# A fused group-norm, channel-attention and box-count kernel: the orders of five engines' half chunks rewritten, VectorE's operations of two units interleaved

## The reference, cut to what matters

```python
# layer 0
x = x + _L0_conv_ref(_gn(x), gamma)     # channel attention: softmax(x^T x), applied to x
# layer 1, on v = _gn(x), scaled to its own least and greatest value
measures = stack([box_sum(v, k) for k in (2, 4, 8, 16)])
log_m    = log(measures + EPS)
alphas   = slope of log_m over log(k)
excite   = sigmoid(relu(mean(alphas) @ w1 + b1) @ w2 + b2)
sim      = cosine of log_m (centred) and the fitted line (centred)
out      = x + sim * sigmoid(batch_norm(alphas)) + (1 - sim) * v * excite
```

## Time and profile before

| | |
|---|---|
| median of 3 runs | 6843.75 us (6843.52 to 6863.24) |
| profiled execution | 6870.93 us, span 6869.2 us |
| busy share of the span: VectorE, TensorE, ScalarE, GpSimd | 80%, 74%, 70%, 26% |
| 32 half chunks of turn 6, first to last L963 | 693.6 us |
| TensorE's mean granted clock | 0.907 of 2.4 GHz |

### The profile page before, as it was taken

The page is one execution under the profiler, slowest core; times in us unless marked ns, Lnnn a source line. Parts: engine busy times, 40 slices in busy tenths (PEclk is TensorE's granted clock), DMA queues, the critical chain, the costliest instruction groups (busy, mean ns, idle before and its releaser), DMA issues. The chain is left out here.

```text
span 6869.2 us, 108733 instructions
## 1 busy us (share of the span) xinstructions
PE 5112.8 (74%) x35320; PEld 4647.5 (68%) x35320; DVE 5524.0 (80%) x6453; ACT 4827.6 (70%) x5203; POOL 1757.7 (26%) x1201
## 2 busy tenths in 40 slices
PE   6968886788858888588867888588885777466643
PEld 6757776677747777477766777477774666466642
DVE  1359998689969999699986999689996999699961
ACT  0118887588848888488875888488884888588861
POOL 0022221422232222322213222322223222333310
PEclk9989998899979999799988999799997999788875
DMA  3635554577746777477755777467774666456656
GB/s 117 195 114 166 176 171 130 176 232 240 230 148 214 226 232 230 132 235 230 223 190 169 238 241 228 148 208 228 236 230 126 219 221 220 159 170 187 189 176 230
DMA packets 874516, 1344.69 MB, mean 196 GB/s; under 512 B 38705, under 2 KB 694097, under 8 KB 857937
## 3 DMA queue, kind: packets, MB, share of 16 engines
q1 hardware_dynamic: 837456, 1208.16, 51.7%
q0 software_dynamic: 36864, 134.23, 10.3%
HBM read 671.16 MB, written 536.87 MB: 176 GB/s over the span
## 5 line engine op out<-in xcount | busy, mean ns | idle before, releaser
L530 PE MATMUL even<-band,t 128*128 128x128 f32 x12288 | 1867.0, 283 | 473.9 <-ACT logs L706 293.3
L530 PEld LDWEIGHTS even<-band,t 128*128 128x128 f32 x12288 | 1625.7, 197 | 548.6 <-issue 444.4
L387 POOL TENSOR_TENSOR t<-t 128x1024 f32<-128x1024 f32 (+3 forms) x800 | 1337.3, 1683 | 1451.3 <-DVE logs L979 1408.3
L511 PE MATMUL h_ps<-mix,xt 128*128 128x256 f32 x4096 | 1054.6, 403 | 454.0 <-DVE mx L891 327.3
L511 PEld LDWEIGHTS h_ps<-mix,xt 128*128 128x128 f32 x4096 | 773.8, 199 | 603.0 <-ACT xt L693 310.7
L428 POOL DMA_DIRECT2D x1t<-logs x256 | 226.4, 884 | 2882.9 <-DVE ut L990 2815.4
L706 ACT ACTIVATE logs<-even,col 128x1024 f32<-128x1024 f32 x512 | 568.8, 1111 | 444.6 <-PE even L530 443.2
L532 PE MATMUL even<-band,t 128*128 128x128 f32 x4096 | 792.0, 275 | 0.0
L891 DVE CUSTOM_DVE_ANT_0 h_out<-h_ps,shift,mx 128x512 f32<-128x512 f32 x512 | 382.7, 748 | 488.5 <-PE h_ps L511 487.5
L488 PE MATMUL g_ps<-xa 128*128 128x257 f32 x2048 | 634.8, 391 | 152.4 <-DMA xa<-in_x_dram 152.1
L532 PEld LDWEIGHTS even<-band,t 128*128 128x128 f32 x4096 | 621.9, 192 | 0.0
(11 more groups left out here) (184 smaller groups left out, 10492.4 us busy)
## 6 DMA issues: line engine op xcount, KB each, us to landing
xa<-in_x_dram SPq DMA_DIRECT2D x256, 512.0 KB, 4.5
xb<-in_x_dram SPq DMA_DIRECT2D x256, 512.0 KB, 5.5
h_scratch<-h_out SPq DMA_DIRECT2D x128, 1024.0 KB, 7.7
hr<-h_scratch SPq DMA_DIRECT2D x256, 512.0 KB, 6.0
q_scratch<-ut SPq DMA_DIRECT2D x256, 512.0 KB, 2.7
x1t<-logs POOLq DMA_DIRECT2D x256, 512.0 KB, 5.1
p_scratch<-x1t SPq DMA_DIRECT2D x256, 512.0 KB, 3.1
pd<-p_scratch SPq DMA_DIRECT2D x256, 512.0 KB, 6.1
```

Of the source, the lines that this page charges most:

```text
L387: ins = g.tensor_tensor(dst[:, hf, d:d + n, :], src[:, hf, d:d + n, :], src[:, hf, e:e + n, :], ALU.add)
L511: ins = t.matmul(h_ps[:, r * C:(r + 1) * C], xt[:, q % 2, jh, r, :], mix[:, jh, :], start=(jh == 0), stop=(jh == 1))
L530: ins = t.matmul(o, src[:, hf, at, :], band[:, which, :], start=True, stop=(which < 3))
```

## The change

Five edits, all in the order of operations or in what they wait for; no operation is added or removed.

1. SyncE: `load_rows` goes ahead of the stores of h and of the output.
2. TensorE: the second `gram_rows` goes from before `box` 3 to behind `turn_back` 0, ahead of the second `mix_x`.
3. ScalarE: order log 0, `copy_xt`, log 2, two squares, log 1, third square, Exp, log 3.
4. VectorE: `norms`, `contrasts` and `finish` are cut into single operations. Each waits for its own producer's count (`dve_done` value handed from one to the other) instead of for the last operation issued. Their order in a half chunk is below.
5. `copy_h` no longer waits for its own end; it waits for the end of the `copy_h` before it, and `min_h` waits for the `copy_h` that it reads. `copy_h` 2 goes behind `high_contrast`; `row_pairs` ahead of the last operation of the tail; `add_slopes` to the next half chunk.

```diff
 # SyncE half_chunk
                     sp.dma_start(pd[:, hf, :], p_dram[ud]).then_inc(pq_loaded[hf], 16)
                     sp.dma_start(qd[:, hf, :], q_dram[ud]).then_inc(pq_loaded[hf], 16)
+                if Cs and not (began and hf == 0) and not (last and (k, hf) != (0, 0)):
+
+                    sp.wait_ge(odd_filled, 2 * u)
+                    apart()
+                    if hf == 1:
+                        load_rows(nC + 2, 1 - k, 0)
+                    else:
+                        load_rows(nC + 1, k, 1)
                 if Bs and hf == 0 and not began:
...
 # TensorE half_chunk
-                if A:
-                    gram_rows(n, hf, 1)
                 if Cs:
                     box(u, k, hf, 3)
...
                 if Ds:
                     turn_back(2 * nd + hf, hf, 0)
+                if A:
+                    gram_rows(n, hf, 1)
                 if Bs:
                     mix_x(nb, 2 * hf + 1)
...
 # VectorE half_chunk
+                v, vf = u - 1, 1 - hf
+                if tail:
+                    two = two_squares(v, vf)
                 if Ds:
                     p_plus_q(nd, 2 * nd + hf, hf)
                 if tail:
-                    norms(u - 1, 1 - hf)
+                    three = three_squares(v, vf, two)
+                if Cs and hf == 0 and tail:
+                    add_slopes(v, 1 - k)
+                if tail:
+                    norm(v, vf, three)
                 if Bs:
                     copy_h(nb, k, 2 * hf, first, 16 * (8 * (s - 1) + i))
                 if Cs:
-                    low_contrasts(u, hf)
+                    low = low_contrasts(u, hf)
+                    high_contrast(u, hf)
                 if Bs:
                     copy_h(nb, k, 2 * hf + 1, first, None)
                 if Cs:
-                    high_contrast(u, hf)
+                    summed = sum_contrast(u, nC, hf, low)
                 if Bs:
-                    min_h(i, k, hf)
-                if Cs:
-                    contrasts(u, nC, k, hf)
+                    min_h(nb, i, k, hf)
                 if tail:
-                    finish(u - 1, 1 - hf)
-                if Cs and hf == 1:
-                    add_slopes(u, k)
+                    similar = similarity(v, vf)
+                if Cs:
+                    cubed = cubic(u, hf, summed)
+                    quadratic(u, hf)
+                    linear(u, k, hf, cubed)
+                if tail:
+                    made = product(v, vf, similar)
...
                 if Cs and not (last and k == 1):
                     row_pairs(k, hf, 16 * (8 * (s - 2) + i + 2), last)
+                if tail:
+                    gated(v, vf, made)
```

More of the change, by code:

```diff
@@ L887, in copy_h @@
                 dve.wait_ge(h_filled, m + 3)
+                dve.wait_ge(h_copied, m + 1)
                 if q == 0 and some(stored):
@@ L939, in low_contrasts @@
                 d.tensor_tensor(L[0], L[0], odd[:, :], ALU.subtract).then_inc(dve_done, own.one())
+                low = own.now()
                 dve.wait_ge(log_ready[2], unit + 1)
                 d.tensor_tensor(L[1], odd[:, :], L[2], ALU.subtract).then_inc(d12_ready, 1)
+                return low
             def high_contrast(unit, hf):
@@ L945, in high_contrast, with sum_contrast, cubic, quadratic @@
                 d.tensor_tensor(logs[:, hf, 2, :], logs[:, hf, 2, :], even[:, :], ALU.subtract).then_inc(d23_ready, 1)
[L947 to L952, removed]
+            def sum_contrast(unit, n, hf, low):
                 if some(16 * n):
                     dve.wait_ge(x1_summed[hf], 16 * n)
[L956 to L959, removed]
+                dve.wait_ge(dve_done, low)
+                dve.wait_ge(d23_ready, unit + 2)
+                d.tensor_tensor(logs[:, hf, 4, :], logs[:, hf, 0, :], logs[:, hf, 2, :], ALU.add).then_inc(dve_done, own.one())
+                return own.now()
+            def cubic(unit, hf, summed):
+                dve.wait_ge(d12_ready, unit + 1)
+                dve.wait_ge(dve_done, summed)
+                d.scalar_tensor_tensor(logs[:, hf, 4, :], logs[:, hf, 1, :], 2.0, logs[:, hf, 4, :], ALU.mult, ALU.subtract
+                                       ).then_inc(dve_done, own.one())
+                return own.now()
+            def quadratic(unit, hf):
+                d.tensor_tensor(logs[:, hf, 0, :], logs[:, hf, 0, :], logs[:, hf, 2, :], ALU.subtract).then_inc(quad_ready, 1)
+            def linear(unit, k, hf, cubed):
                 at = 2 * hf + k
-                d.scalar_tensor_tensor(L[1], L[4], -0.3, L[1], ALU.mult, ALU.add, accum_out=slope[:, at:at + 1]
-                                       ).then_inc(slopes, 1)
-                d.tensor_tensor(L[0], L[0], L[2], ALU.subtract).then_inc(quad_ready, 1)
+                dve.wait_ge(dve_done, cubed)
+                d.scalar_tensor_tensor(logs[:, hf, 1, :], logs[:, hf, 4, :], -0.3, logs[:, hf, 1, :], ALU.mult, ALU.add,
+                                       accum_out=slope[:, at:at + 1]).then_inc(slopes, 1)
             def add_slopes(unit, k):
@@ L969, in add_slopes, with two_squares, three_squares @@
                 dve.wait_ge(dve_done, own.now())
-            def norms(unit, hf):
-                z = logs[:, hf, 4, :]
+            def two_squares(unit, hf):
                 dve.wait_ge(squares, 3 * unit + 2)
-                d.tensor_tensor(z, z, logs[:, hf, 3, :], ALU.add).then_inc(dve_done, own.one())
+                d.tensor_tensor(logs[:, hf, 4, :], logs[:, hf, 4, :], logs[:, hf, 3, :], ALU.add).then_inc(dve_done, own.one())
+                return own.now()
+            def three_squares(unit, hf, two):
@@ L975, in norms @@
                 dve.wait_ge(squares, 3 * unit + 3)
[L976 to L982, removed]
-                dve.wait_ge(inv_ready, unit + 1)
[L984 to L988, removed]
+                dve.wait_ge(dve_done, two)
@@ new lines, in three_squares, with norm, similarity @@
+                d.tensor_tensor(logs[:, hf, 4, :], logs[:, hf, 4, :], logs[:, hf, 0, :], ALU.add).then_inc(dve_done, own.one())
+                return own.now()
+            def norm(unit, hf, three):
+                dve.wait_ge(dve_done, three)
+                d.tensor_tensor(logs[:, hf, 4, :], logs[:, hf, 4, :], logs[:, hf, 3, :], ALU.mult).then_inc(z_ready, 1)
+            def similarity(unit, hf):
+                dve.wait_ge(inv_ready, unit + 1)
+                d.tensor_tensor(logs[:, hf, 3, :], logs[:, hf, 3, :], logs[:, hf, 4, :], ALU.mult).then_inc(dve_done, own.one())
+                return own.now()
@@ L989, in finish, with product, gated @@
+            def product(unit, hf, similar):
+                dve.wait_ge(dve_done, similar)
+                d.tensor_tensor(logs[:, hf, 4, :], logs[:, hf, 1, :], logs[:, hf, 3, :], ALU.mult).then_inc(dve_done, own.one())
+                return own.now()
+            def gated(unit, hf, made):
+                dve.wait_ge(dve_done, made)
                 dve.wait_ge(x1_ready, unit + 2)
-                d.scalar_tensor_tensor(ut[:, hf, :], sim, -1.0, ut[:, hf, :], ALU.add, ALU.mult).then_inc(tail_done, 1)
+                d.scalar_tensor_tensor(ut[:, hf, :], logs[:, hf, 3, :], -1.0, ut[:, hf, :], ALU.add, ALU.mult).then_inc(tail_done, 1)
@@ L1052, in turn @@
                 if Cs:
-                    norms(u - 1, 1)
+                    two = two_squares(u - 1, 1)
+                    add_slopes(u - 1, 1)
+                    norm(u - 1, 1, three_squares(u - 1, 1, two))
                 if A:
@@ L1057, in turn @@
                 if Cs:
-                    finish(u - 1, 1)
+                    gated(u - 1, 1, product(u - 1, 1, similarity(u - 1, 1)))
                 if A:
```

16 lines of the change are left out of this document (4 added, 12 removed).

## The result

The changed kernel takes 6629.48 us (median of 4 runs, 6622.28 to 6632.39) against 6843.64 before (4 runs, 6837.24 to 6863.24): a ratio of 0.968, 95% interval 0.966 to 0.970. The forecast was 6533, the range 6430 to 6700. The profiled execution took 6632.39 us.

A forecast was written before the change was run, and what follows sets the result against it. VectorE's chain was taken to bound the kernel, afterwards a loop through xa. Turns 3 to 7 -251, turn 2 -38, turn 8 -28, turn 9 +6: -311 on 6871 gives 6560, less 27 for the median 6533 us; range 6430 to 6700.

The forecast's parts named there:

- What bounds the kernel: Turns 3 to 7: VectorE's own chain, 21.15 us of a 22.37 us half chunk, the other 1.2 being waits.
- VectorE's order: Fewer dependent neighbours and waits save 0.87 us a half chunk; a 0.15 us `sum_contrast` stall leaves VectorE alone at 20.43.
- SyncE: Half 0: hr, issued ahead of both stores, lands before them and VectorE's wait for it goes, net -0.8 us.
- TensorE: Moving the second `gram_rows` into the idle before the second `mix_x` removes its slow run: -0.5 us per half chunk.
- ScalarE: Box 2 lies open, cycle 20.3 us, level with VectorE; without the move VectorE would wait for the squares.
- The loop over two half chunks: From `gated` through x1 DMA, p store, xa load and squares back to `gated`: 41.4 us, period 20.75 in turns 3 to 7.
- rival 2: Waits stay as large as now, 1.2 us: period 21.6 in turns 3 to 7, 6677 us; chance 0.17.
- Turns 2 and 8: Turn 2 without p_plus_q: period 20.1, -38 us; turn 8 without xa: VectorE's 20.45, -28 us.
- Between the turns: Statistics between turns, with fill and drain: 0, same operations in the same places; bounds -10 to +20 us.
- the loop isn't closed: Xa lands in time, VectorE and ScalarE alone set period 20.43 in turns 3 to 7: 6459 us; chance 0.17.
- the order saves nothing: VectorE's chain stays 21.15 and only waits go, period 21.3 in turns 3 to 7: 6655 us; chance 0.08.
- the slower one: Xa landing 8.8 us after issue closes the loop, period 22.9 in turns 3 to 7: 6946 us; chance 0.06.

The follow-up runs named there:

- e2: Kernel before with only the SyncE, TensorE and ScalarE moves, VectorE's block as before: 6714 us, ratio 0.979.
- e11: e5 with `min_h` ahead of `sum_contrast` again, as in the kernel before: 6454 us, ratio 0.942 to the kernel before.
- e8: Changed kernel with the load of hr back behind the stores of h and of the output: 6928 us, ratio 1.011 to the kernel before.
- e7: Changed kernel with TensorE's second `gram_rows` ahead of box 3 as before: 6657 us, ratio 0.970 to the kernel before.
- e1: Kernel before with only VectorE's new order and waits, the other three engines as before: 6969 us, ratio 1.016.
- e6: Changed kernel with ScalarE's order as before, squares ahead of `copy_xt` and log 2: 6688 us, ratio 0.976 to the kernel before.
- e9: Changed kernel plus one matmul of zeros ahead of the first `gram_rows` in turns 2 to 7: 6584 us, ratio 0.962 to the kernel before.
- e10: Changed kernel plus one matmul of zeros ahead of box 2 in turns 8 and 9: 6587 us, ratio 0.962 to the kernel before.
- e5: e3 with ScalarE's x1t parted from ut and put behind log 0: 6478 us, ratio 0.945 to the kernel before.
- e3: Changed kernel with TensorE's first `gram_rows` behind box 0 instead of ahead of it: 6503 us, ratio 0.948 to the kernel before.
- e12: e3 with eight VectorE operations also waiting for the operation just ahead: 6694 us, ratio 0.978 to the kernel before.

## Why the prediction was right, and where it was off

- **In all**: the chain named as the bound, the loop that ends last and the direction were right. The gain was forecast at 311 us and is 238.5 on the profiled execution. The misses are -194 for -251 in turns 3 to 7, -18 for -38 in turn 2, -12 for -28 in turn 8, and -20 for 0 between the turns. The last makes good part of the others by luck. The 27 us taken off for the median were the old kernel's; the new profiled execution lies 3 above its median. So the medians differ by 214 us where 311 were forecast.
- **What bounds the kernel**: right. VectorE's chain was the floor, before (e2: 21.26 with hardly a wait, forecast for the chain 21.15) and after (20.41 of 20.43).
- **VectorE's order**: the size was right, by two errors that cancel. The stall of `sum_contrast` behind GpSimd was put at 0.15 and is 0.41 (1.63 - 1.22). The wait behind `copy_h` saved 0.31 and not 0.1: from `copy_h` to the next operation 0.86 and 0.79 before, 0.67 and 0.68 after. The test named for this ("wrong if L956's mean is over 1.6 us outside turn 9") is at its line: 1.63 in turns 3 to 7, 1.57 over turns 2 to 8. e11 takes the stall away.
- **SyncE**: the term was right (-0.8 forecast, from 0.79 to 0.08 found), but it was priced against the kernel before. In the new kernel the edit holds up some 300 us (e8).
- **TensorE**: the slow `mix_x` did go, but not by this edit alone. It is gone without it too (e7), while with the interleaving alone 41 of 155 are slow (e1), so the moves of SyncE and ScalarE, or one of them, remove it. The 0.5 a half chunk that was booked here is not what the edit is worth (e7: 0.07, within noise).
- **ScalarE**: the cycle was right (20.23 against 20.3). The reason given for the move, that VectorE would otherwise wait for the squares, was wrong (e6): log 2, box 3 and `mix_x` would be late.
- **The loop over two half chunks**: the term that was mis-sized is its length, 2T = 41.4 and T = 20.75 with jitter, where the period is 21.13. The chain up to xa is nearly as forecast, 11.25 us from the end of `gated` to xa's landing (mean of 29 in turn 6; 11.4 over turns 3 to 7; forecast 11.3). Too small was "3.4 us" for `gram_rows` 0 and box 0, at full clock: in 19 of 155 half chunks they follow 2 us of idle and run at 1.2 GHz, up to 1.3 us and more longer. The prediction had said that the idle might return elsewhere and priced it only where it was. By e9 (20.88) that is 0.25 a half chunk, 38 us, and less by e10. The other 0.13 is not shown by any run; the single turns vary by more (20.96 to 21.33), and three engines at 20.2 to 20.4 with DMA that varies could explain it. 0.05 was taken for this; rival 2 saw it and put it at 1.2, far too high.
- **One test named beforehand is open to two readings**: "wrong if VectorE's longest wait is the squares or the similarity by over 1 us". The longest wait is the squares', 0.64 us a half chunk on the mean where 0.3 was forecast, but up to 2.9 us in one (15 waits of 1.4 us in turn 6). Read by single waits the test is failed, read by the mean it is passed. Either way the loop costs twice what was forecast: VectorE's 20.41 to 21.13, and not 20.43 to 20.75.
- **Turns 2 and 8**: turn 8's box 2 runs slow behind 2.8 us of idle. Without that the period is 20.36 to 20.42 (e10, e5) for 20.98; the forecast, 20.45, had box 2 at full clock. Turn 2 came at 20.77 instead of 20.1; e3 gives 19.53 there, so the xa loop was closed in it too, and was longer than the sum made it. Only one `gram_rows` 0 of 31 is slow there, so it is not the clock. Its length there wasn't taken apart.
- **Between the turns**: 20 us came that were forecast as 0, beyond the bound of -10. The same stretches fall from 723.5 to 708 us in e1 and to 717 in e2, so more of it goes with the interleaving than with the moves. Which operations in them gain isn't known.
- **The rivals**: that the loop isn't closed is out by e3, that the order saves nothing by e12, and the slower one (a late xa) by xa's landing, whose median is 4.6 us for 4.5.

## What to carry to other kernels

When a change shortens the bounding engine's chain, price every load and every partner's order against the new, shorter period first: the interleaving alone lost 1.6%, and with the other moves but without the moved load the kernel still lost 1.1%. A queue that is in order makes loops that no engine's busy time shows (a load behind a store behind a DMA behind the last operation); write out such a loop in full, and look for the consumer that is cheapest to move. When TensorE is left idle ahead of a piece on the path, look up a row of that piece at the lower clock and price how often it may come; work that is moved into one gap can open another. Before a difference of 0.4% is put down to an edit, find it in the trace: a wait, a stall or a count that changed.

## What the runs showed of the hardware that was not expected

- The kernel with one more matmul of zeros in TensorE's idle time ahead of `gram_rows` 0 is 45 us faster than without (e9); in turns 3 to 7, where the matmul stands, 38 us of the profiled executions' 55 are gained. There the pieces behind it run at 2.4 GHz in all 155 half chunks, where 19 of them ran at 1.2 GHz.
- Two builds with the same instructions in turns 3 to 7 (changed kernel and e10) differ by 0.14 us in the period, and have 19 and 9 slow starts.
- `sum_contrast`, whose two inputs lie in SBUF, ends 1.08 to 1.09 us behind GpSimd's operation in all 216 cases of the changed kernel in which it is long; its mean is 1.63 us for 1.22 alone. Its row shows no idle time, so the stall is found by the duration only. `copy_h` and the contrasts that read PSUM keep their durations beside the same GpSimd operations (0.75, and 1.21 to 1.22 us), and so does `min_h` in e11 (1.22 us, 150 times).
